# Row copies issued in an earlier block, and projections spread among maxima, in a two-layer decoder kernel

## The reference

```python
# layer 0, self-attention: 16 blocks of 128 tokens, 16 "heads" of 16 features each,
# a head's rows being a reshape (not a transpose) of the block, q, k, v in bfloat16
xc = conv(x);  xs = xc + xc @ pe_w.T
qkv = (xs @ qkv_w.T).reshape(b, s, 3, d)
attn = softmax(q @ k.T / sqrt(hd));  o = attn @ v

# layer 1, cross-attention: 16 heads of 16 features, keys and values from the context
q = x @ w_q + b_q;  k = context @ w_k + b_k;  v = context @ w_v + b_v
out = softmax(q @ k.T / 4) @ v;  out @ w_o + b_o
```

## Time and profile before

| | |
|---|---|
| median of 3 executions | 3531.74 us |
| the three executions | 3519.54, 3531.74, 3532.99 us |
| the profiled execution | 3519.54 us, of which span 3517.8 us |
| busy in the span | PE 3188.8, DVE 2359.7, POOL 1711.4, ACT 1706.0 us |
| layer 0 self-attention, second block | about 70.6 to 710 us |
| layer 1 cross-attention | about 2624.5 to 3323 us |

### The profile page before, as it was taken

One profiled execution on the slowest core, in us unless ns is written; L12 is line 12 of the kernel. 1 busy time (PEld: TensorE's weight loads), 2 busy tenths in 40 slices (PEclk: granted clock), 3 DMA queues, 4 the chain that ended last, 5 costly groups with the idle time before them and its releaser, 6 DMA issues. The chain is left out here.

```text
span 3517.8 us, 63984 instructions
## 1 busy us (share of the span) xinstructions
PE 3188.8 (91%) x24265; PEld 1814.3 (52%) x24265; DVE 2359.7 (67%) x5271; ACT 1706.0 (48%) x2086; POOL 1711.4 (49%) x1145
## 2 busy tenths in 40 slices
PE   7999999989999999999999935869989999999797
PEld 4666666644555555555555514845545434444346
DVE  5999999945655665665566564155427978888528
ACT  1888888833434444434444431222223766666641
POOL 4888888814777777776777811201351000000012
PEclk9999999999999999999999967979997999999899
DMA  2100000020000000000000064620012111111101
GB/s 59 39 2 2 2 2 2 2 54 1 4 1 4 1 4 4 1 3 1 4 1 1 1 201 131 173 69 1 1 27 33 18 17 18 18 18 18 33 1 36
DMA packets 62584, 88.35 MB, mean 25 GB/s; under 512 B 9457, under 2 KB 52338, under 8 KB 61426
## 3 DMA queue, kind: packets, MB, share of 16 engines
q1 hardware_dynamic: 59250, 80.27, 9.0%
q0 software_dynamic: 3072, 4.34, 0.7%
HBM read 61.28 MB, written 8.54 MB: 20 GB/s over the span
## 5 line engine op out<-in xcount | busy, mean ns | idle before, releaser
L922 DVE TENSOR_REDUCE x0hm<-x0pM 128x1 f32<-128x400 f32 (+1 forms) x1024 | 520.3, 561 | 378.1 <-PE x0pM L824 378.0
L403 POOL TENSOR_SCALAR rows<-rows,mb 128x1024 bf16<-128x1024 bf16 x512 | 567.4, 1119 | 113.0 <-DVE mb L355 113.0
L349 DVE TENSOR_SCALAR_CACHE_REDUCE rows<-pS 128x1024 bf16<-128x1024 f32 x512 | 616.7, 1205 | 0.9 <-PE pS L298 0.9
L414 ACT ACTIVATE prT<-pP 128x1024 bf16<-128x1024 bf16 x512 | 523.3, 1024 | 116.3 <-PE pP L309 115.9
L1386 DVE TENSOR_REDUCE x1hm<-x1pM 128x1 f32<-128x400 f32 (+1 forms) x1024 | 518.6, 566 | 69.4 <-PE x1pM L1272 66.0
L1505 ACT ACTIVATE x1pr<-x1pST 128x1024 f32<-128x1024 f32 (+1 forms) x416 | 403.8, 1022 | 218.0 <-PE x1pST L1324 217.9
L784 POOL TENSOR_TENSOR x0acc<-x0acc,x0pr 128x1024 f32<-128x1024 f32 (+1 forms) x176 | 421.4, 2394 | 110.8 <-ACT x0pr L1033 95.0
L784 POOL TENSOR_TENSOR x0acc<-x0acc,o_nat 128x1024 f32<-128x1024 f32 (+1 forms) x176 | 419.2, 2382 | 72.0 <-ACT o_nat L1033 53.2
L1033 ACT ACTIVATE x0pr<-x0pST 128x1024 f32<-128x1024 f32 (+1 forms) x208 | 212.9, 1024 | 279.4 <-PE x0pST L868 279.1
L1033 ACT ACTIVATE o_nat<-x0pST 128x1024 f32<-128x1024 f32 (+1 forms) x208 | 213.0, 1024 | 278.5 <-PE x0pST L868 277.9
L1272 PE MATMUL x1pM<-x1sk,x1sq 64*128 64x400 f32 (+1 forms) x1024 | 321.8, 443 | 14.9 <-DVE x1ql L1377 4.1
(11 more groups left out here) (362 smaller groups left out, 5156.5 us busy)
## 6 DMA issues: line engine op xcount, KB each, us to landing
m_w<-in_moe_w1T SPq DMA_DIRECT2D x16, 1024.0 KB, 10.5
m_w<-in_moe_w2T SPq DMA_DIRECT2D x16, 1024.0 KB, 7.0
x1sq<-x1qh SPq DMA_DIRECT2D x32, 128.0 KB, 4.0
x1sk<-x1kh SPq DMA_DIRECT2D x32, 100.1 KB, 3.6
rows_d<-m_xr SPq DMA_DIRECT2D x1, 2176.0 KB, 7.8
acc_d<-m_zero SPq DMA_DIRECT2D x4, 514.0 KB, 6.8
m_acc<-acc_d SPq DMA_DIRECT2D x4, 514.0 KB, 6.8
g_xN<-in_x SPq DMA_DIRECT2D x1, 2048.0 KB, 8.5
```

The lines of the kernel that those rows point to most:

```text
L349: nc.vector.tensor_scalar(rows[u][:, half * 1024:(half + 1) * 1024], pS[half][:, :], 1.0, None, ALU.mult, ALU.max, accum_out=mx[u][:, half ...
L403: nc.gpsimd.tensor_scalar(r, r, -1.0, mb[u][:, 0:1], ALU.mult, ALU.add).then_inc(s_df, 1)
L414: nc.scalar.activation(prT[u][:, half * 8:(half + 1) * 8, :], pP[half][:, :, :], ACT.Exp, scale=-1.0 / HD ** 0.5).then_inc(s_ex, 1)
L922: emptied(nc.vector.tensor_reduce(hm[g % 2][:, a, t, i % 8 // 2:i % 8 // 2 + 1], bank(name)[:, 0:w], AX.X, ALU.max, negate=True), name)
```

## The change

Four edits.

1. `qp` and `kp` are allocated with the first block's own tensors, so their memory ends with it.
2. The 48 row copies of the rest move on SP from the head of block two to the end of block one.
3. Of the 13 units v in layer 1, four stay ahead of the maxima (`V_EARLY`). The other nine stand among the maxima: after maxima 1, 5, 9, ..., 33.
4. In `stack`, SP waits for all eight units q and k before its first DMA, and alternates the pieces of `sk` and `sq`, half by half.

```diff
                     rows_of(sp, "k", range(16), first, s_first)
+                    sp.wait_ge(s_q, 8)
+                    rows_of(sp, "q", range(16), rest, s_rest)
+                    sp.wait_ge(s_k, 8)
+                    rows_of(sp, "k", range(16), rest, s_rest)
...
                 @block.sync
                 def _(sp):
-                    sp.wait_ge(s_q, 8)
-                    rows_of(sp, "q", range(16), rest, s_rest)
-                    sp.wait_ge(s_k, 8)
-                    rows_of(sp, "k", range(16), rest, s_rest)
                     sp.dma_start(G.xN[:, :, :], ...).then_inc(G.s_x, 16)
...
+    V_EARLY = 4
...
-    first = [(x, 0, r) for x in ("q", "k") for r in range(4)] + [("v", t) for t in range(NC_)]
+    first = [(x, 0, r) for x in ("q", "k") for r in range(4)] + [("v", t) for t in range(V_EARLY)]
     first_maxima = []
     for i in range(done(-1, 0)):
         first_maxima.append(("max", i))
+        if i % 4 == 1 and V_EARLY + i // 4 < NC_:
+            first_maxima.append(("v", V_EARLY + i // 4))
...
+                    for x in ("k", "q"):
+                        for r in range(4):
+                            wait_emptied(sp, (x, j // 4, r))
                     if j >= 2:
                         sp.wait_ge(s_st, 4 * STEPS * (j - 1))
-                    for x, dst, parts in (("q", sq[j % 2], (qh, qh, ql)), ("k", sk[j % 2], (kh, kl, kh))):
-                        for r in range(4):
-                            wait_emptied(sp, (x, j // 4, r))
-                        for a in range(2):
...
+                    for a in range(2):
+                        mine = slice(32 * (j % 4) + 16 * a, 32 * (j % 4) + 16 * a + 16)
+                        sp.dma_start(sq[j % 2][64 * a + 48:64 * a + 49, :].bitcast(F32), zero[:, :])...
+                        for dst, parts in ((sk[j % 2], (kh, kl, kh)), (sq[j % 2], (qh, qh, ql))):
```

More of the change, by code:

```diff
@@ L83, in l0_attention_heads @@
         v1 = m.sb("v1", [P, NT, 16, HD + 1], BF16)
-        qp = m.sb("qp", [P, DJ, T], BF16)
-        kp = m.sb("kp", [P, DJ, T], BF16)
         s_zero, s_one = m.sem("c_zeroed"), m.sem("c_one")
         s_first, s_rest = m.sem("c_rows_first"), m.sem("c_rows_rest")
[L89 to L92, removed]
-                    for a in range(2):
[L94 to L99, removed]
         with ExitStack() as c1:
@@ L107, in l0_attention_heads @@
             wqkv = m1.sb("wqkv", [P, DJ, 3 * D])
+            qp = m1.sb("qp", [P, DJ, T], BF16)
+            kp = m1.sb("kp", [P, DJ, T], BF16)
             pA = [m1.ps(f"pA{i}", [P, 512]) for i in range(6)]
@@ L135, in wait_bank, with rows_of @@
                     wait_emptied(eng, order[place[unit] - 6])
+            def rows_of(queue, x, cs, cols, sem):
+                for c in cs:
+                    mine = slice(16 * (c % 8), 16 * (c % 8) + 16)
+                    if x == "q":
+                        for a in range(2):
+                            queue.dma_start(qT[64 * a:64 * a + HD, c, cols], qp[mine, c // 8, cols]).then_inc(sem, 16)
+                    else:
+                        a, spot = c % 8 // 4, 4 * (c // 8) + c % 4
+                        queue.dma_start(kT[64 * a:64 * a + HD, spot, cols], kp[mine, c // 8, cols]).then_inc(sem, 16)
+            first, rest = slice(0, 512), slice(512, T)
             with nc.Block() as block:
@@ L1190, in stack @@
                     sp.wait_ge(s_row, 5 if j == 0 else 9)
+                    for x in ("k", "q"):
+                        for r in range(4):
+                            wait_emptied(sp, (x, j // 4, r))
                     if j >= 2:
                         sp.wait_ge(s_st, 4 * STEPS * (j - 1))
-                    for x, dst, parts in (("q", sq[j % 2], (qh, qh, ql)), ("k", sk[j % 2], (kh, kl, kh))):
-                        for r in range(4):
-                            wait_emptied(sp, (x, j // 4, r))
[L1197 to L1201, removed]
+                    for a in range(2):
+                        mine = slice(32 * (j % 4) + 16 * a, 32 * (j % 4) + 16 * a + 16)
+                        sp.dma_start(sq[j % 2][64 * a + 48:64 * a + 49, :].bitcast(F32), zero[:, :]).then_inc(s_stack[j % 2], 16)
+                        for dst, parts in ((sk[j % 2], (kh, kl, kh)), (sq[j % 2], (qh, qh, ql))):
                             for i, part in enumerate(parts):
```

## The result

| | before | changed |
|---|---|---|
| median, four executions each | 3531.61 us | 3582.59 us |
| lowest and highest | 3519.54, 3532.99 | 3567.90, 3586.25 |
| profiled execution, its span | 3519.54, 3517.8 | 3560.77, 3559.0 |

The changed kernel takes 1.0144 times as long, with a 95% interval of 1.0108 to 1.0180. "Slower" was forecast, but the time lies 8.6 us above the range and 20.6 above the 3562 that was named. Between the two profiled executions the difference is 41.2 us, where 30.8 was forecast, and these two traces account for it in three places. Their own times are 3519.54 and 3560.77; the medians, 51.0 us apart, come for the most part from executions without a trace.

A forecast was written before the change was run, and what follows sets the result against it. DVE was taken to bound layer 0's attention, and PE layer 1 after the 76 maxima. The terms 20.1 + 4.5 + 6.2 = 30.8 us, added to the median 3531.74, gave 3562 us, range 3540 to 3574.

The forecast's parts named there:

- Slower: Whole kernel: slower than before by over 0.5%, chance 0.84.
- row copies at the border: Layer 0: SP's 48 moved issues make it reach the border late, so the attention starts later: +20.1 us.
- stack: Layer 1 cross-attention: the first stack DMA also waits for the last k, so the maxima start later: +4.5 us.
- v among the maxima: Layer 1: DVE idles at each of nine v, two at half clock and seven at full: +6.2 us.
- the rival that it does not: Layer 0 border: others are not held for SP's issues, so only 10.7 us are lost, 3542.4 us; chance 0.07.
- The rival of the fast queue: SP's queue at both heads: issues under 0.51 us per DMA, ending at "not slower"; at 0.35, 3539.8 us; chance 0.04.
- The row for the low end: Layer 0 border: 48 copies at the pace of the first 48, 31.3 us, giving a loss of 18.2 us.
- my own prices: Layer 1 maxima: DVE idle time per v, 0.46 us at full clock and 1.5 us at half clock.
- the chain: Layer 1: from a bank's release through the v to DVE's next maximum, 1.43 us at full clock, 2.47 at half.
- the upper bound of 13.5: Layer 1 maxima: high end of the loss, all nine v at half clock, 1.5 us each.
- 1.2 GHz for all nine v: Layer 1 maxima: PE stays at half clock, 13.5 us for the v, sum 38.1, so 3569.8 us; chance 0.14.

The follow-up runs named there:

- edits 1 and 2 alone: The kernel before with only the 48 row copies moved ahead of the border and qp, kp allocated with the first block: 3538.42 us against 3520.96, ratio 1.0050.
- twenty copies: The kernel before with 20 of the 48 row copies moved ahead of the border instead of all: 3525.31 us, one execution.
- half the pause: The kernel before with only the nine units v spread among the maxima, SP's stack unchanged, so PE pauses 6.5 us instead of 13.8: 3538.32 us, ratio 1.0054.
- the pause filled by work: The changed kernel with 16 repeated v projections, result overwritten, on PE while it waits for the stack: 3572.11 us, one execution.
- eight maxima: The changed kernel with one v to every eight maxima in place of one to every four: 3574.77 us, one execution.
- a bank of its own: The changed kernel with the nine late v in the two banks of the scores instead of the maxima's three: 3574.91 us, one execution.
- finer pieces: The changed kernel with late v in banks of their own, each cut in two parts of its contraction, one to every two maxima: 3575.53 us, one execution.
- edit 4 alone: The kernel before with only SP's stack waiting for all q and k units and alternating its pieces: 3534.05 us, ratio 1.0011.
- the first tap on ACT: The kernel before with the convolution's first tap on ACT instead of DVE: 3522.04 us against 3521.79, ratio 0.9988.

## Why the prediction failed

The sum was 30.8 us by three terms. By the traces:

| term | forecast | its bounds | measured |
|---|---|---|---|
| row copies at the border | 20.1 | 18.2 to 20.5 | 17.5 |
| stack | 4.5 | 2.7 to 5.4 | 6.0 |
| v among the maxima | 6.2 | 0 to 13.5 | 18.2 |

*Reading the bound: right.* DVE bounds the attention and gives nothing back; PE bounds the rest of layer 1 and gives nothing back. The border does hold the others for SP's issues: the rival that it does not falls with edits 1 and 2 alone, and twenty copies, with which SP is not late, cost nothing. The rival of the fast queue falls too: 30.7 us for 48 issues is 0.64 each, not under 0.51.

*The border's size: a little too large.* I took the pace of the copies in block two, 33.2 us for 48. Away from the attention they took 87.27 - 56.58 = 30.7, about what the first 48 had taken (31.3). The 17.5 lies below the low bound of 18.2 too. The row for the low end was the nearer one: same block, same neighbours.

*The stack's size: a little too small.* Of the 6.0 us, the first DMA is 2660.89 - 2645.09 = 15.80 after the first unit q instead of 10.26, 5.5 later, not 5.36. The last issue began 2671.50 - 2660.89 = 10.61 after the first (10.85 before), which is as forecast. From there to PE's start it took 5.6 us, not the 4.0 of the earlier trace rows; 1.21 of it is the issue itself, twice the usual length. I had also taken the row of `x1qh`, though the last piece is one of `x1ql`, for which the DMA view of the kernel before has 4.4. Where the rest of the 1.6 comes from stays open.

*The step that failed: the v among the maxima.* Its +6.2 us ("the first two v at half clock, seven at full") were 18.2. It has two faults, both shown. The prediction's own sign for it, 76 maxima that take over 10 us more than before, is what came.

First the clock. I read from the earlier trace rows that PE regains its pace soon after a pause, and carried that from dense projections to a mixture with maxima, although had the maxima alone let the clock fall to 0.50 with PE at 31.95 of 32 us. All nine ran at 1.2 GHz. It wasn't the pause: with half the pause the groups are the same, and with the pause filled by work the clock falls within the mixture. By my own prices, seven v at 1.5 in place of 0.46 are 7.3 of the 12.0 us by which the term was short.

Second the price of a v at 1.2 GHz: 1.5 forecast, 2.07 measured (4.00 - 1.93). I began the chain at the bank that the v itself takes, 0.07 ahead of its start, with two maxima as cover. By the experiments with eight maxima and with a bank of its own it begins one maximum earlier, with three as cover: 0.06 + 0.63 - 0.48 = 0.21 where I had 0.07. The v holds PE for 2.00 and not 1.74: I had doubled 0.87, the pace of v behind v, and among maxima a v takes 1.07 at 2.4 GHz as well. The next maximum takes 0.74 and not 0.66. Together 0.48, and 0.09 more because DVE needs 2.02 and not 1.93 for four maxima after standing idle. Nine times the difference of 0.57 is 5.1 us; the first v, behind two maxima only, cost 0.4 less, which makes 7.3 + 5.1 - 0.4 = 12.0. (At 2.4 GHz the price was short as well: 0.46 forecast, 0.72 measured.) So the upper bound of 13.5 was no bound. It was the value of one chain at the lower clock, with no room for longer links, and the earlier trace rows had timed the v at 2.4 GHz only. The rival "1.2 GHz for all nine v", given 0.14, is the one that held, at 18.2 in place of its 13.5.

*From the profile to the median.* On the profiled execution's own time the forecast was 3550.3 and it took 3560.8; these 10.4 us are the three terms (-2.6, +1.5, +12.0, and -0.5 elsewhere). The other 10 us between 3562 and 3582.59 lie between executions, not in the trace: on the second chip the same kernel's median was 3572.74. With the three terms as measured the forecast would have been 3531.74 + 41.2 = 3572.9, at the upper edge of the range but inside it; what put the median outside is this part, which no trace shows. What may set some of it is in the last section; why three of the four executions of the first chip lie at 3581 to 3586 stays open.

*Granularity or spacing.* Spacing does nothing (1.98 idle per v at four and at eight maxima), finer pieces win 3.7 us, the bank nothing. Pieces with eight maxima between them were not tried.

## What to carry to other kernels

DMA issues placed ahead of an all-engine border cost the time by which they make the issuing queue the last to arrive; count them at the pace of the same queue in the same block. Work inserted on an engine between short pieces that another engine consumes costs what it outlasts the buffered pieces by, hand-over on both sides included: here 3.43 us against 1.45 buffered. So put it where its engine waits anyway: here the nine v were free ahead of the maxima, where they covered the stack's transfers. Before costing TensorE work at full clock, look at the granted clock of the stretch it moves into, and give the slower clock the main forecast where the trace shows it: here 0.50 with PE busy 31.95 of 32 us.

## What was unexpected of the hardware

**A stall at the head, in some executions.** DVE's first two instructions (`xc<-xp,cw`, fp32, operands in SBUF), before, and in the kernel with edit 4 alone:

```profile
5.14 1.85 DVE L169 TENSOR_SCALAR xc<-xp,cw 128x512 f32<-128x512 f32 x2 [5.14 <-DMA cw<-in_conv]
```

```profile
5.55 18.62 DVE L169 TENSOR_SCALAR xc<-xp,cw 128x512 f32<-128x512 f32 x2 [5.55 <-DMA cw<-in_conv]
```

In the second they end at 24.17, 0.9 us after POOL's run of memsets of qT and kT, which ends at 16.13 + 7.16 = 23.29 (POOL's timeline, edits 1 and 2 alone, where DVE is stalled alike, until 24.14):

```profile
1.63 14.57 POOL L162 MEMSET qT<- 128x1024 f32 x16
16.13 7.16 POOL L164 MEMSET kT<- 128x1024 f32 x8
```

The attention of layer 0 then ends about 14.4 us later (p0wv at 725.2 in place of 710.8). In traces without the stall the sixteen memsets of qT take 15.69 us in place of 14.57: there it is POOL that is slowed. Among stalled executions the moved copies also cost a little more than 17.5 us: p0wv is at 743.0 to 744.1 with them, and at 724.8 and 725.2 without. SCALAR_TENSOR_TENSOR isn't held by the memsets: with the first tap on ACT, eight of them take 5.41 us beside them, 0.68 each. There the upper group of times is gone too, as it should be if the stall makes it. Which of the timed executions were stalled is not known, so neither is how large a part of the difference between medians comes from unequal shares of them.

The Trainium skill (SBUF — State Buffer, who interferes with whom) says that VectorE and GpSimd share a port pair as an exclusive lock, that `tensor_scalar` can enter the modes that take it, and that whoever issues second is blocked fully, not slowed, for the length of the other's instruction. The traces agree in kind: of the twelve of kernels that start so, four have 1.8 to 2.3 us and eight 18.3 to 19.2, nothing between. They show more than one instruction's length, though: a memset takes 0.9 us, and DVE waits through the whole run of them. What decides between the two cases isn't shown.

**The clock falls under a busy PE.** In the kernel with work in the pause it went from 1.00 to 0.50 within 2700 to 2704 with PE busy 3.59 us of four ahead of that and 3.78 in it. It then stayed at 0.50 under the mixture; in the kernel with the v in two pieces it did so with PE busy 4.00 us of four, and in the kernel before under the maxima alone with 31.95 of 32. So a PE that the profile shows as full can be at 1.2 GHz. The Trainium skill (TensorE: Matmul & The Clock Gate, HAM oscillation) puts such falls down to bursts of work between which PE stands idle for a DMA. No wait of that kind is in these rows: PE idles for some tenths of a microsecond at a time, and it waits for DVE and ACT to empty banks. Which property of the mixture lets the clock fall, the narrow maxima (64 of 128 rows), their pace or the short idle gaps, was not separated.
